# A perceiver block with routed experts on one core: the order ahead of the first routed slot laid out anew, and two shared-expert units moved around the last slot

## The reference

```
x = x + xattn(layernorm(x), ctx)        # softmax over 1601 keys, one head of 256
x = x + attn(layernorm(x))              # causal over the 64 tokens
h = layernorm(x)
raw = h @ centroids.T                   # 8 routed experts
balanced = sigmoid(raw + routing_bias)  # the top 2 are chosen by this
w = softmax(sigmoid(raw)[top 2])
x = x + h + sum over 2 shared experts of gelu(h @ Wfc.T) @ Wproj.T
          + sum over the 2 chosen experts of w * gelu(h @ Wfc.T) @ Wproj.T
```

## Time and profile before

| | us |
|---|---|
| median of 3 runs | 261.04 (259.86 to 261.11) |
| the profiled execution: its time | 261.1 |
| its span in the trace | 259.3 |
| TensorE busy | 246.6 |
| VectorE busy | 153.6 |
| ScalarE busy | 136.8 |
| GpSimd busy | 46.9 |

### The profile page before, as it was taken

One profiled execution on the slowest core, in us unless ns is written; L12 is line 12 of the kernel. 1 busy time (PEld: TensorE's weight loads), 2 busy tenths in 40 slices (PEclk: granted clock), 3 DMA queues, 4 the chain that ended last, 5 costly groups with the idle time before them and its releaser, 6 DMA issues.

```text
span 259.3 us, 5119 instructions
## 1 busy us (share of the span) xinstructions
PE 246.6 (95%) x1908; PEld 210.6 (81%) x1908; DVE 153.6 (59%) x374; ACT 136.8 (53%) x265; POOL 46.9 (18%) x77
## 2 busy tenths in 40 slices
PE   8999899999999799978999999999999999999993
PEld 8757536366366579968999989999999999999992
DVE  1832334454745759748783535666677777776764
ACT  1225205152154475996855826666666666666650
POOL 5100000000100001004107600231211222126520
PEclk9999799999999999999999999999999999999998
DMA  7999999999997999910802237899999999951052
GB/s 255 428 424 365 429 423 436 385 421 404 379 373 268 325 316 409 433 83 0 306 21 78 88 102 250 280 348 373 350 362 349 351 351 357 362 240 43 20 162 81
DMA packets 14254, 74.12 MB, mean 286 GB/s; under 512 B 1524, under 2 KB 8956, under 8 KB 9884
## 3 DMA queue, kind: packets, MB, share of 16 engines
q1 hardware_dynamic: 12700, 70.59, 72.1%
q0 software_dynamic: 1008, 2.76, 2.8%
q10 hardware_dynamic: 528, 0.52, 0.6%
HBM read 67.56 MB, written 6.32 MB: 285 GB/s over the span
## 4 chain that ended last, share of the span: by engine, by line
PE 72%; DMA 9%; ACT 7%; DVE 6%; issue 2%; SPq 1%; POOL 0%; DVEq 0%; ACTq 0%
PE psum L500 62%; DMA rows<-rows_dram 9%; PE psum L746 5%; PE psum L589 2%; ACT L928 1%; ACT hraw L928 1%; ACT whi L911 1%; PE psum L768 1%; ACT hhi L932 1%; DVE stats L1020 1%; DVE xn L1027 1%; PE psum L811 1%; PE psum L636 1%; DVE xs L1144 1%; ACT L894 0%
## 5 line engine op out<-in xcount | busy, mean ns | idle before, releaser
L500 PE MATMUL psum<-xrowT,ring 128*128 128x128 f32 x480 | 58.4, 275 | 0.6 <-DVE xrowT L1289 0.6
L500 PEld LDWEIGHTS psum<-xrowT,ring 128*128 128x128 f32 x480 | 56.2, 192 | 0.8 <-issue 0.8
L1297 DVE TENSOR_TENSOR dlo<-ring,dhi 128x1024 fp32r<-128x1024 f32 x30 | 37.1, 1235 | 4.6 <-ACT dhi L952 4.6
L1316 DVE TENSOR_TENSOR slot_hlo<-slot_h,slot_hhi 128x512 fp32r<-128x512 f32 x30 | 20.8, 692 | 29.3 <-ACT slot_hhi L980 29.3
L978 ACT ACTIVATE slot_h<-psum 128x512 f32<-128x512 f32 x30 | 18.0, 600 | 36.0 <-PE psum L500 36.0
L500 PE MATMUL psum<-dhi,slot_hhi 128*128 128x256 f32 x120 | 36.3, 302 | 0.1
L500 PE MATMUL psum<-dhi,slot_hlo 128*128 128x256 f32 x120 | 33.8, 282 | 0.0
L500 PE MATMUL psum<-dlo,slot_hhi 128*128 128x256 f32 x120 | 33.8, 282 | 0.0
L952 ACT ACTIVATE dhi<-ring 128x1024 fp32r<-128x1024 f32 x30 | 31.2, 1040 | 0.0
L492 POOL DMA_INDIRECT results_dram<-y_rows,result_row x13 | 16.9, 1301 | 69.8 <-DMA results_dram<-y_rows,result_row 54.6
L500 PE MATMUL psum<-ctx,probT 128*64 128x256 f32 (+1 forms) x208 | 25.5, 392 | 0.0
(11 more groups left out here) (198 smaller groups left out, 443.7 us busy)
## 6 DMA issues: line engine op xcount, KB each, us to landing
ring<-experts_dram SPq DMA_DIRECT2D x15, 2048.0 KB, 7.8
ctx<-ctx_dram SPq DMA_DIRECT2D x4, 3072.0 KB
ctxT_start<-ctxT_start_dram SPq DMA_DIRECT2D x4, 2048.0 KB, 17.9
ctxT_rest<-ctxT_rest_dram SPq DMA_DIRECT2D x4, 1154.0 KB, 20.3
raw<-experts_dram SPq DMA_DIRECT2D x2, 2048.0 KB, 13.8
slot_x_dram<-empty_row SPq DMA_DIRECT2D x1, 1935.0 KB, 14.3
xrow<-slot_x_dram SPq DMA_DIRECT2D x15, 129.0 KB, 7.2
squares<-squares_dram SPq DMA_DIRECT2D x1, 1285.0 KB, 14.4
```

The source lines that it names most:

```text
L500: return pe.matmul(out, lhsT, rhs, start=first, stop=last)
L1297: dve.tensor_tensor(dlo[b % 2][:, steps, :], ring[b][:, steps, C * P:STEP_W], dhi[b % 2][:, steps, :].bitcast(F32), ALU.subtract).then_inc ...
L1316: dve.tensor_tensor(slot_hlo[:, half, :], slot_h[:, half, :], slot_hhi[:, half, :].bitcast(F32), ALU.subtract).then_inc(slot_hlo_ready, 1)
```

## The change

Five edits:

1. The list for the last tile is laid out anew. Hidden ("hid"), stage ("feat") and down are names of their own, so that they can stand anywhere. In W of the last tile 8 steps stand ahead of xn2T, and no unit stands in W.
2. The units are numbered expert by expert: both halves of the tokens for expert 0, then both for expert 1. High and low parts of the weights lie side by side in one buffer, `parted`.
3. Units 30 and 31 (TAIL) are taken out of the list. The hidden half of 30 runs in the last slot behind its first down half, that of 31 behind its second; the two down halves stand around the two halves of combine(1).
4. The bias row is added to `mix` later: the copy out of PSUM waits for nothing but the product, and the sum with `rows` is made in bias_folds. The load of `rows` moves behind both ctxT loads of tile 1.
5. The sum x + h is no longer made by VectorE in norm3 but by GpSimd behind the 8 scatters; the last 65 keys of ctx have a semaphore of their own; `lsum2` has two columns.

```diff
-              ("proj", c), ("norm3", late), ("norm2", c), ("split", 0), ("W", t, 0, 3), ("split", 1),
-              ("xn2T", c), ("xn3T", late), ("W", t, 3, 6), ("split", 2), ("split", 3), ("tq", c), ("W", t, 6, 9),
...
-              ("unit", 28), ("unit", 29), ("unit", 30), ("unit", 31), ("slot_rows", )]
+              ("proj", c), ("W", t, 0, 1), ("split", 0), ("norm3", late), ("W", t, 1, 2), ("norm2", c),
+              ("W", t, 2, 4), ("split", 1), ("split", 2), ("split", 3), ("split", 4), ("W", t, 4, 8), ("xn2T", c),
...
+              ("feat", 27), ("down", 25), ("down", 26), ("hid", 29), ("slot_rows", ), ("down", 27), ("feat", 28),
+              ("down", 28), ("feat", 29), ("down", 29)]
...
+            for t in range(T):
+                pool.tensor_tensor(xs[:, t, :], xs[:, t, :], xn[:, t, 0:D], ALU.add).then_inc(x3_ready, 1)
...
             load_ctx(0)
+            load_ctxT(1)
             sp.dma_start(rows[:, :], rows_d.partition_broadcast(P)).then_inc(rows_in, 16)
-            load_ctxT(1)
...
-            return (n // J) % SHARED, n % J, n // (SHARED * J)
+            return n // (2 * J), n % J, (n // J) % 2
...
                 else:
-                    combine(0)
+                    unit_hidden(UNITS - 2)
+                    combine(0, range(T))
                 slot_down(slot, b, 1)
...
-            combine(DIRECT - 1)
+            unit_hidden(UNITS - 1)
+            unit_down(UNITS - 2)
+            combine(1, range(2))
+            unit_down(UNITS - 1)
+            combine(1, range(2, T))
...
-            dve.wait_ge(rows_in, 16)
-            dve.tensor_tensor(mix[:, :], bank(PO, 0, D), rows[:, 0:D], ALU.add).then_inc(fold_dve, 1)
+            dve.tensor_copy(mix[:, :], bank(PO, 0, D)).then_inc(fold_dve, 1)
...
+                dve.wait_ge(rows_in, 16)
+                link(dve.tensor_tensor(mix[:, :], mix[:, :], rows[:, 0:D], ALU.add))
...
-                link(dve.tensor_tensor(xs[:, t, :], xs[:, t, :], xn[:, t, 0:D], ALU.add))
```

More of the change, by code:

```diff
@@ L38 @@
 UNITS = 2 * SHARED * J
+TAIL = 2
 XWQT, XWKT, XWVT, XWO, AWQ, AWK, AWVT = range(7)
@@ L772, in _ @@
                     "xn2T": chain_xn2T, "tq": chain_tq, "sc": chain_scores, "v": chain_v,
-                    "probT": chain_prob2T, "z": chain_z, "xn3T": chain_xn3T, "lead": unit_hidden,
-                    "unit": unit, "route": route, "rank": ranks, "slot_rows": lambda: slot_rows(0, 1)}
+                    "probT": chain_prob2T, "z": chain_z, "xn3T": chain_xn3T, "hid": unit_hidden,
+                    "down": unit_down, "route": route, "rank": ranks, "slot_rows": lambda: slot_rows(0, 1)}
             for what, *args in ORDER:
@@ L803, in slot_down, with combine @@
                     ins.then_inc(slot_down_ps, 1)
-            def combine(n):
+            def combine(n, tiles):
                 pe.wait_ge(places_ready, n + 1)
-                for part, ready, done in ((last_hi, last_hi_ready, False), (last_lo, last_lo_ready, n == DIRECT - 1)):
+                for part, ready in ((last_hi, last_hi_ready), (last_lo, last_lo_ready)):
                     pe.wait_ge(ready, n + 1)
-                    for t in range(T):
+                    for t in tiles:
                         ins = pe.matmul(bank(SHARED_BANK + t // 2, (t % 2) * D, D),
                                         places[:, n, t * P:(t + 1) * P], part[:, n, :],
-                                        start=False, stop=done, skip_group_check=True)
-                        if part is last_lo and t % 2 == 1:
-                            ins.then_inc(combined_ps, 1)
+                                        start=False, stop=n == DIRECT - 1 and part is last_lo, skip_group_check=True)
+                ins.then_inc(combined_ps, 1)
             def slot_step(slot, b, n, last=False):
@@ L966, in _ @@
             mine = {"T": probT_copy, "exp": exps, "xn2T": xn2T_copy, "tq": tq_copy, "exp2": exp2,
-                    "probT": prob2T_copy, "xn3T": xn3T_copy, "split": split, "unit": unit,
-                    "lead": stage, "sigmoid": route, "gates": gates,
+                    "probT": prob2T_copy, "xn3T": xn3T_copy, "split": split,
+                    "feat": stage, "sigmoid": route, "gates": gates,
                     "slot_down": first_split_down}
@@ L1301, in _ @@
                     "norm2": norm2, "norm3": norm3,
-                    "tq": c2_dot, "sc": softmax2, "v": v_copy, "z": x2_add, "xn3T": split_x,
+                    "tq": c2_dot, "sc": softmax2, "v": v_copy, "z": x2_add, "xl": split_x,
                     "split": lambda q: split_low(q, q % J, q // J % 2),
-                    "unit": unit, "lead": stage, "sigmoid": route, "top2": top2,
+                    "feat": stage, "rz": route, "top2": top2,
                     "indices": indices, "hot": mark, "choices": choices, "place": place,
@@ L1339, in slot_step @@
                 else:
-                    for k in range(TOP):
-                        add_picked(k)
+                    add_picked(0)
+                    stage(UNITS - 2)
+                    add_picked(1)
                 if direct is not None:
```

107 lines of the change are left out of this document (55 added, 52 removed).

## The result

| | before | changed |
|---|---|---|
| median of 4 runs each, us | 261.08 (259.86 to 263.71) | 253.41 (252.87 to 255.16) |
| profiled execution: time | 261.1 | 252.87 |
| its span | 259.3 | 251.1 |
| TensorE busy | 246.6 | 242.7 |
| VectorE, ScalarE, GpSimd busy | 153.6, 136.8, 46.9 | 153.5, 135.5, 50.2 |

The ratio is 0.9736, with a 95% interval from 0.9695 to 0.9777: faster, by 7.7 us between the medians and by 6.9 us by the ratio, where 5.05 were predicted. Executions with a second, disturbed state of the chip are left out of the ratios, and of the counts of executions by their clock further down.

A forecast was written before the change was run, and what follows sets the result against it. TensorE was taken as the bound nearly everywhere, so gains could come only from waits ahead of slot 0, the clock and the end. From 261.1, -6.8 up to slot 0 and +1.75 at the end gave 256.0 us, range 253.6 to 259.4.

The forecast's parts named there:

- waits between W and slot 0: TensorE's waits from W's end to slot 0 fall from 4.5 to 3.7 us, a gain of 0.8.
- rows wait: Tile 1: probT's copy no longer waits for rows; nb and T come 0.9 us sooner, with 0 for the clock.
- stop in W: W of the last tile: TensorE's 1.50 us stop for xn goes, worth -1.5, with 0 as the other bound.
- W in fewer groups: W of the last tile, cut into three groups instead of five, gives 0.8 us; called the least certain piece.
- four halves from ahead of slot 0: Ahead of slot 0: 60 halves instead of 63 and a hidden one in W, worth 2.8 us.
- the end: Last slot's first down half to VectorE's last sum: 7.3 us instead of 5.56, so +1.75.
- the six that the prediction followed: W's end to slot 0: waits of 0.65, 0.4, 1.0 (z), 0.5, 0.85 and 0.3 us, together 3.7.
- more falls away: Rival, chance 0.15: table loads start ahead of their data, clock stays up, waits fall from 3.7 to 1.5, giving 253.8 us.
- Is slot 0 fed: Ahead of slot 0: its rows come in at about 140.5, TensorE wants them at 142.6, so hidden by 2 us.
- x + h on GpSimd: Behind the scatters: four sums priced at up to twice the copies, stretch covered by VectorE's idle time; 0.8 us without cover.
- The end and the two units: Last slot: end +1.75 against 2.8 for the moved halves, so filling the last wait gains 1.05 us.

The follow-up runs named there:

- 1: Kernel before with only the rows edit (later load of rows, sum with rows made in bias_folds): 260.26 us, ratio 0.9995.
- 2: Kernel before, unaltered, profiled a second time: 259.34 us, one execution.
- 7: Kernel before with the rows edit and eight steps of W ahead of xn2T of the last tile, not three: 259.31 us, ratio 0.9959.
- 4: Changed kernel with units 30 and 31 back in the list ahead of slot 0: 254.41 us, ratio 0.9777.
- 5: Changed kernel with units 30 and 31 back in the list ahead of slot 0, run again on another chip: 253.84 us, ratio 0.9751.
- experiment 6: Changed kernel with the old list for the last tile and old unit order, units 30 and 31 still around the last slot: 262.35 us, ratio 1.0083.
- first group: Follow-up runs on one chip, each beside runs of the kernel before, which took 259.94 us there (23 runs).
- third group: Follow-up runs on another chip than the first group, beside the kernel before at 260.99 us (11 runs) and the unaltered changed kernel at 252.75 us.

## Why the prediction was right in sign and short in size

What it said of the direction, and where the time would come from, held: nearly all of it ahead of slot 0, some of it given back at the end. The step that failed is the term of the sum for the waits between W and slot 0: 3.7 us were put down, and 1.1 to 1.4 were there. That is the 2.6 us by which the forecast is too long and the range missed. The rows term, too, came out near its number by luck. Step by step, against the profile of before, which the sum starts from:

| step | predicted | shown |
|---|---|---|
| rows wait | -0.9 | -1.3 in the profile, all of it the clock's; 0 at the median (1, 2) |
| stop in W | -1.5 | stop gone; alone half is lost to new stops (7) |
| W in fewer groups | -0.8 | about -0.45 |
| waits between W and slot 0 | -0.8 | about -3.0 to -3.4 |
| four halves from ahead of slot 0 | -2.8 | -1.75 and -2.2, net of stops that come or grow without them (4, 5) |
| the end | +1.75 | +1.5 |

The new stops are in the row of the waits already; with -2.8 for the four halves the column comes to -7.6 to -8.0, and the spans differ by 8.2.

**The rows wait** failed too, in its mechanism. The prediction held that `nb`, and with it T of tile 1, comes 0.9 sooner because the copy of probT no longer stands behind `rows`, and took 0 for the clock. It was the other way about. In the earlier trace rows the maxima end with TensorE's scores, and these were late by the fall of the clock; in the execution of before without it `nb` starts at 38.52, which is 0.5 earlier than with the edit. The edit moves the wait for `rows` into the chain to `nb`, as the prediction's own arithmetic said (its 34.9 for `rows` was 34.6, its 39.45 for `nb` was 39.15), and what it gives is the clock. That T of tile 1 came 1.3 sooner than in the first profile, not far from the 0.9, is luck. The row with 0.83 was there to be asked what the kernel would do without the fall.

**The waits 4.5 to 3.7** are the term that made the forecast 2.6 us too long. The changed kernel takes 143.01 - 88.15 = 54.86 us from W's end to slot 0. Less the predicted 42.3 for 60 halves and 11.5 for small pieces, 1.1 are left, not 3.7. The same subtraction on the rows edit alone, 151.01 - 93.27 = 57.74 less 44.4 and 8.9, gives 4.4, but that only repeats how the prediction had split the stretch, as its 8.9 was what the 4.5 left over. Two readings do not hang on the split. The idle time that the profile shows fell from 3.5 to 0.98. And where two matmuls in a row start over 0.35 us apart, instead of about 0.12, the excess adds up to 4.4 in six places before and to 1.4 in three now. So the waits fell by 3.0 to 3.4. The largest that is left, the 0.62 for `hlo`, is not among the six that the prediction followed; and of those six none can be seen, since from 88.2 to 106.8 TensorE is idle for 0.10 in all, and behind it the two named stops are 0.83 of the 0.88. An example:

```profile
102.73 0.26 ACT L913 ACTIVATE prob2T<-psum 128x128 f32<-128x128 f32 x1
```

This is ScalarE's timeline in the changed kernel at the place of the longest of them, z, priced at 1.0. Behind a table load and a stage the copy of prob2T was made from 102.73 to 102.99; the timeline of TensorE has z at 103.28, with no idle time behind a down half and two transposes:

```profile
103.07 0.38 PE L692 MATMUL psum<-ident,xn 128*128 128x128 f32 x2
103.28 0.60 PE L512 MATMUL psum<-v,prob2T 128*128 128x256 f32 x2
```

The estimate added the latencies of ScalarE's queue and set them against a TensorE that it had come too early: each wait was priced as if the one ahead of it had not yet held TensorE up or had been filled by a half. Small waits in a row would then be covered by the same halves of 0.7 us. This reading of the arithmetic is argued, and no run tests it; that the six are absent is shown. The rival "more falls away", with 1.5 of waits and 253.8, was the nearer one, and as it said, the table loads stop nobody.

**W.** The mark came at 88.15, predicted 88.3. Between T of the last tile and W's end the changed kernel takes 10.15 us, where the rows edit alone takes 15.40. Of the 5.25, 2.6 are the small pieces that went behind W and 0.7 the hidden half; 1.95 are left, the stop of 1.5 and 0.45, where 0.8 had been put down for fewer groups. Experiment 7 shows that with the old order behind W half of the stop comes back in three others; that it is worth its full 1.5 with the rest of the list rests on this sum.

**Is slot 0 fed.** `xrow` was predicted at 140.5 and came at 140.55, by errors that cancel, which is luck. The prediction let the rows follow the load of ring buffer 1, issued at 132 and landed 7.8 later. The load was issued 3.5 sooner, at 128.51. But it also delayed the last scatter, which landed at 137.62, 6.72 after its issue, and the rows took 2.93 more. `rows_of` was done at 120.0, not 122.8 (a sum in which 14.3 stands where the text has 13.8), since the waits were shorter. TensorE was there sooner as well, at 140.4 and not 142.6, so the 2 us of cover became a wait of 0.21. That the cover depends on the list is what experiment 6 shows.

**x + h on GpSimd.** Priced at nothing, and it is worth nothing: 252.92 against 253.02. The stretch on VectorE, 2.1 us, is larger than the 0.8 that stood as the price without cover. The Trainium skill ("SBUF — State Buffer", Who interferes with whom) says that a VectorE instruction with two SBUF inputs contends with a GpSimd one that reads SBUF, and that such contention is an exclusive lock. The trace agrees that they contend: each of the two dlo is 0.69 longer, over half of a GpSimd sum (0.39 in the second profile of experiments 4 and 5), which the stretch of `hlo` beside the copies, 0.18, had not suggested. That one stands for the whole of the other's instruction is not shown.

**The end and the two units.** Predicted 7.3 and a net of 1.05; measured 7.1, and 1.1 by the times, with intervals that overlap. The profiles show less, 0.2 to 0.7.

**The sum again.** On the chip of the first group, from before to the rows edit +0.3, to the new list -5.85, to the units around the last slot -1.1 (third group): 253.3, where the changed kernel, in other groups, had 253.41, 252.92 and 252.75. Not tried by themselves were the numbering of the units, the semaphore for the last 65 keys and `lsum2`. That the weights lie interleaved changes nothing on TensorE: in the chain of waits of the changed kernel 18 matmuls of down halves take 2.14, 0.71 to six, as in the earlier trace rows.

```profile
141.03 2.14 PE psum L760 x18
```

## What to carry to other kernels

Before a stretch is used as the base of a sum, look at its granted clock, and if it has fallen, profile the unaltered kernel again: here one and the same kernel had T of tile 1 at 42.99 and at 41.28, and a difference of 1.3 us between two profiles was nearly put down to an edit that moves nothing at the median.

Work taken from ahead of a transfer's consumer is only gained if the transfer comes earlier too. The four halves were worth up to 1.1 us with the new list; with the old list, and everything else changed, the kernel was slower than before, since a wait of 2.5 took their place and the clock fell behind it.

When waits are followed through a list, do not simply add them: here six came to 3.7 us, and none of them was seen. Give the term a range from nothing to the waits of before, 4.5 here. Its middle would have been 2.2 here, still above the 1.1 to 1.4 that came; that this helps in another kernel is not shown.

## What was not expected of the hardware

- The fall of the clock ahead of T of tile 1 was there in one profile of the kernel before and not in the other, with nearly the same waits ahead of it (5.40 us of VectorE and 1.00 of TensorE in the one with it, 5.24 and 0.84 in the one without). By their mean clocks 21 of 46 executions of that kernel had it, and these take 1.6 us more.
- Behind a wait of 2.53 us in the profile of experiment 6 the clock was at 1.2 GHz for about 7 us, at 0.60 of full speed on average from 150 to 158. That is 3 us lost on top of the wait, in one of the two worst of twelve executions.
- A scatter of GpSimd's issued 2.4 us behind a load of 2 MB on SyncE's queue landed after 6.7 us; with that load issued later after at most 2.5, and with it long done after 2.95 (experiment 6).
- Sums of 128x256 from SBUF took 1.21 us each on GpSimd beside a busy VectorE, where VectorE takes 0.43, and made two VectorE instructions of 128x1024 beside them 0.69 longer each, in another profile 0.39.
